# Routing and scattering one group ahead of the shared experts in a transformer-block kernel

## What is computed

```python
shared_out = einsum(silu(x @ shared_gate) * (x @ shared_up), shared_down)   # every token, width 256
router_probs = softmax(x @ router)                                          # 8 experts
topk_probs, topk_idx = top_k(router_probs, 2)
...
expert_out = (silu(x @ experts_gate[e]) * (x @ experts_up[e])) @ experts_down[e]
routed = sum over the two chosen experts of prob * expert_out
return routed + shared_out                                                  # x is the layer norm of the stream
```

## Time and profile before

| | before |
|---|---|
| median of 3 runs | 942.51 us |
| lowest, highest | 940.07, 943.23 us |
| the profiled execution, its own time | 942.55 us |
| its span, first to last instruction | 940.7 us |
| mean granted clock of TensorE | 0.942 |
| expert groups, first routing product to the first quad transpose | 234.3 to 379.48 us |

### The profile page before, as it was taken

How to read it: one execution, slowest core, us unless ns; L and a number is a source line. 1 busy time by engine, 2 the same in 40 slices (tenths; PEclk the granted TensorE clock), 3 DMA queues, 4 the chain that set the end, 5 groups by cost and what they waited for, 6 DMA issues and landing times. The chain is left out here.

```text
span 940.7 us, 24231 instructions
## 1 busy us (share of the span) xinstructions
PE 825.0 (88%) x9252; PEld 687.1 (73%) x9252; DVE 720.6 (77%) x1407; ACT 628.3 (67%) x1170; POOL 577.6 (61%) x666
## 2 busy tenths in 40 slices
PE   5699999998988786788888859999998889999995
PEld 4588888887867676778887748888877745555663
DVE  3699998887755655557565478999989968999996
ACT  2488888875633420656555128988787759999995
POOL 2355878653335344155555478879998877777551
PEclk9799999999989988799889959999999989999997
DMA  8500111000112115455443386500110320004000
GB/s 261 104 3 2 48 47 36 3 2 2 45 51 84 60 69 184 123 149 176 142 147 123 129 290 92 88 6 3 23 27 2 46 36 18 29 24 84 29 29 28
DMA packets 48481, 66.88 MB, mean 71 GB/s; under 512 B 10097, under 2 KB 36337, under 8 KB 48369
## 3 DMA queue, kind: packets, MB, share of 16 engines
q1 hardware_dynamic: 31520, 36.97, 13.3%
q0 software_dynamic: 15232, 27.80, 11.7%
q10 hardware_dynamic: 1616, 0.58, 0.3%
HBM read 35.04 MB, written 26.10 MB: 65 GB/s over the span
## 5 line engine op out<-in xcount | busy, mean ns | idle before, releaser
L568 POOL TENSOR_TENSOR sm_a<-sm_a,mx_a 128x1232 f32<-128x1232 f32 x64 | 144.0, 2250 | 84.4 <-DVE mx_a L968 84.2
L1258 POOL DMA_INDIRECT mixed<-rep,qidx_f x80 | 79.5, 994 | 82.9 <-DVE rep L1770 62.8
L968 DVE TENSOR_REDUCE mx_a<-sm_a 128x16 f32<-128x1232 f32 x64 | 91.9, 1436 | 2.2
L735 PE MATMUL pT_a<-ident,pr_a 128*128 128x128 f32 x640 | 92.1, 275 | 1.1 <-ACT pr_a L869 1.1
L869 ACT ACTIVATE pr_a<-sm_a 128x1232 f32<-128x1232 f32 x64 | 79.0, 1235 | 12.0 <-POOL sm_a L568 12.0
L1252 POOL DMA_INDIRECT slots<-sx,idx_f x48 | 47.3, 985 | 64.4 <-DVE idx_f L1656 51.6
L735 PEld LDWEIGHTS pT_a<-ident,pr_a 128*128 128x128 f32 x640 | 75.0, 142 | 2.9 <-ACT pr_a L869 1.9
L759 PE MATMUL pA_a<-aw,ot_a 128*128 128x256 f32 x256 | 66.2, 381 | 0.9 <-DVE x L986 0.9
L1949 PE MATMUL pS<-b,dg 128*128 128x512 f32 x124 | 60.2, 609 | 4.0 <-PEq L446 4.0
L961 DVE TENSOR_TENSOR sm_a<-pS_a,mask 128x1232 f32<-128x1232 f32 x32 | 46.1, 1441 | 11.7 <-PE pS_a L721 9.1
L750 PE MATMUL pO_a<-rep,V 128*32 128x128 f32 x1024 | 52.2, 276 | 1.6 <-DVE ot_a L981 1.6
(11 more groups left out here) (356 smaller groups left out, 2681.4 us busy)
## 6 DMA issues: line engine op xcount, KB each, us to landing
sx<-slots SPq DMA_DIRECT2D x40, 272.0 KB
x<-x_in SPq DMA_DIRECT2D x4, 1024.0 KB, 11.4
x<-mixed POOLq DMA_DIRECT2D x4, 1024.0 KB, 10.0
out_x<-x SPq DMA_DIRECT2D x32, 128.0 KB, 1.7
rep<-gu_in SPq DMA_DIRECT2D x10, 256.0 KB, 2.9
slots<-zeros_f SPq DMA_DIRECT2D x9, 272.0 KB
aw<-aw_in SPq DMA_DIRECT2D x2, 1024.0 KB, 7.2
ha<-mixed SPq DMA_DIRECT2D x2, 1024.0 KB, 7.4
```

Of the source, the lines that this page charges most:

```text
L568: pool.tensor_tensor(heads, heads, mx[u][:].rearrange("p (h a) -> p h a", a=1).broadcast_to([P, HEADS, SK]), ALU.subtract).then_inc(shifte ...
L735: mm = pe.transpose(pT[:, (J * t + j) % 2, (n % 4) * P:(n % 4 + 1) * P], pr[u][:, g, c * P:(c + 1) * P], sb["ident"][:])
L968: dve.tensor_reduce(mx[u][:], sm[u][:].rearrange("p (h k) -> p h k", k=SK), AX.X, ALU.max).then_inc(maxed, 1)
L1258: pool.indirect_dma_start(dram["mixed"][:], bass.IndirectOffsetOnAxis(qidx[:, at:at + 1], 0), ys[q % 2][:, j, :], None).then_inc(out_moved ...
```

## The change

Routing and scattering are moved one group ahead of the shared experts. Period s now holds the shared experts of s, the turning of s+2, and the ranking, finding and addresses of s+1; the routing product of s+2 ends it. In a longer opening, groups 0 and 1 are both routed beside shared group 0. The last period has shared work alone. For that there are three sets of turned rows and four of rows to scatter. The third turned set and the rows' middle two lie where the quads' weights `wb` come later, so ACT waits for the scatters of groups 5 and 6 before the second copy. The weights of quads 0 and 1 are copied before the quads begin. SP's zero fills are moved ahead of its waits for group 6. DVE computes the table before the products of group 7, and makes the columns `bvb` behind the last `add`. The filler calls between the last down products are gone; the 14 behind them remain. `choose` is split into `rank_of` and `choose`.

```diff
@@ -37,7 +37,7 @@
 AHEAD = 2
-THIRDS = 3
+ROWSETS, XSETS = 4, 3
 NG = T // ST
@@ -1163,8 +1163,11 @@
 qidx = sbt("qidx", [P, NQ * ST], mybir.dt.uint32)
-with nc.sbuf_tensor("rows_third" + tag, [P, ST, ROW], F32) as third:
-    rows = [*sx, third]
+with ExitStack() as groups:
+    own_set = lambda n, shape, d: groups.enter_context(nc.sbuf_tensor(n + tag, shape, d))
+    xh, xl = ([sb[n + "_first"], second, own_set(n + "_third", [P, G, GW], F32R)]
+              for n, second in (("xh", xh_second), ("xl", xl_second)))
+    rows = [sx[0], *(own_set(n, [P, ST, ROW], F32) for n in ("rows_second", "rows_third")), sx[1]]
 wb = pair("wb", [P, 2, 2 * G * D], F32R)
@@ -1209,12 +1212,12 @@
-    sp.sem_inc(rows_free, THIRDS * ST)
+    sp.sem_inc(rows_free, ROWSETS * ST)
     for g in range(NG):
-        if g == NG - 1:
+        if g == NG - 2:
             tails()
         for j in range(ST):
-            sp.wait_ge(moved[g % THIRDS][j], 16 * TOPK * (g // THIRDS + 1))
+            sp.wait_ge(moved[g % ROWSETS][j], 16 * TOPK * (g // ROWSETS + 1))
             sp.sem_inc(rows_free, 1)
@@ -1289,7 +1293,8 @@
-    def find(g, u, last=False):
+    def find(g, last=False):
+        u = g % 2
         pe.wait_ge(sel_ok, g + 1)
@@ -1329,35 +1334,52 @@
-    def group(s, u):
-        turn(s + 1, 0)
-        gate_up(s, u, 0, 1)
-        gate_up(s, u, 1, 0)
-        turn(s + 1, 1)
-        gate_up(s, u, 1, 1)
-        find(s, u)
-        turn(s + 1, 2)
+    def turn_ahead(s, j):
+        if s + 2 < NG:
+            turn(s + 2, j)
+
+    def group(s):
+        turn_ahead(s, 0)
+        gate_up(s, 0, 0)
+        if s + 1 < NG:
+            route_back(s + 1)
+        gate_up(s, 0, 1)
+        turn_ahead(s, 1)
+        gate_up(s, 1, 0)
+        turn_ahead(s, 2)
+        gate_up(s, 1, 1)
+        if s + 1 < NG:
+            find(s + 1, s + 2 == NG)
         down(s, 0)
-        turn(s + 1, 3)
+        turn_ahead(s, 3)
         down(s, 1)
-        route(s + 1, 1 - u)
-        gate_up(s + 1, 1 - u, 0, 0)
-        route_back(s + 1)
-
-    route(0, 0)
+        if s + 2 < NG:
+            route(s + 2)
+
+    route(0)
+    turn(1, 0)
     pe.wait_ge(sb["split_low"], PIECES)
-    gate_up(0, 0, 0, 0)
+    gate_up(0, 0, 0)
     route_back(0)
-    for s in range(NG - 1):
-        group(s, s % 2)
-    gate_up(NG - 1, 1, 0, 1)
-    gate_up(NG - 1, 1, 1, 0)
-    find(NG - 1, 1, True)
-    gate_up(NG - 1, 1, 1, 1)
-    keep_busy(pe, sb, pX, 4)
-    down(NG - 1, 0)
-    keep_busy(pe, sb, pX, 10)
-    down(NG - 1, 1)
+    turn(1, 1)
+    gate_up(0, 0, 1)
+    turn(1, 2)
+    find(0)
+    turn(1, 3)
+    route(1)
+    turn(2, 0)
+    gate_up(0, 1, 0)
+    route_back(1)
+    turn(2, 1)
+    gate_up(0, 1, 1)
+    find(1)
+    turn(2, 2)
+    down(0, 0)
+    turn(2, 3)
+    down(0, 1)
+    route(2)
+    for s in range(1, NG):
+        group(s)
     keep_busy(pe, sb, pX, 14)
@@ -1487,36 +1510,59 @@
     def norm_ahead(s, j):
+        if s + 3 < NG:
+            norm(s + 3, j)
+
+    def high_ahead(s, j):
         if s + 2 < NG:
-            norm(s + 2, j)
-
-    def group(s, u):
-        x_high(s + 1, 1 - u, 0)
+            x_high(s + 2, j)
+
+    def group(s):
+        if s + 1 < NG:
+            logits_out(s + 1)
+        high_ahead(s, 0)
+        norm_ahead(s, 0)
         silu(s, 0)
-        soft(s)
-        norm_ahead(s, 0)
-        x_high(s + 1, 1 - u, 1)
+        high_ahead(s, 1)
+        if s + 1 < NG:
+            soft(s + 1)
         high(s, 0)
+        high_ahead(s, 2)
+        norm_ahead(s, 1)
         silu(s, 1)
-        norm_ahead(s, 1)
-        x_high(s + 1, 1 - u, 2)
+        norm_ahead(s, 2)
         high(s, 1)
-        norm_ahead(s, 2)
-        x_high(s + 1, 1 - u, 3)
+        high_ahead(s, 3)
         norm_ahead(s, 3)
-        logits_out(s + 1)
...
     logits_out(0)
+    x_high(1, 0)
     for j in range(1, ST):
         norm(1, j)
-    for s in range(NG - 1):
-        group(s, s % 2)
-    silu(NG - 1, 0)
-    soft(NG - 1)
-    high(NG - 1, 0)
-    silu(NG - 1, 1)
-    high(NG - 1, 1)
+    x_high(1, 1)
+    silu(0, 0)
+    soft(0)
+    x_high(1, 2)
+    high(0, 0)
+    norm(2, 0)
+    norm(2, 1)
+    x_high(1, 3)
+    norm(2, 2)
+    norm(2, 3)
+    logits_out(1)
+    x_high(2, 0)
+    x_high(2, 1)
+    soft(1)
+    silu(0, 1)
+    x_high(2, 2)
+    high(0, 1)
+    norm(3, 0)
+    x_high(2, 3)
+    for j in range(1, ST):
+        norm(3, j)
+    for s in range(1, NG):
+        group(s)
@@ -1545,11 +1591,18 @@
             quad_high(q + 2, u, 1)
-            gate_up_weights(q + 2, u)
+            if q >= 0:
+                gate_up_weights(q + 2, u)
         if has(1):
...
     act.wait_ge(table_ok, 1)
+    gate_up_weights(0, 0)
+
+    for g in (NG - 3, NG - 2):
+        for j in range(ST):
+            act.wait_ge(moved[g % ROWSETS][j], 16 * TOPK * (g // ROWSETS + 1))
+    gate_up_weights(1, 1)
     run_quads(step)
@@ -1611,6 +1665,9 @@
         dve.tensor_reduce(rank[:], gt[:], AX.X, ALU.add).then_inc(r_chain, 1)
+
+    def choose(g):
+        r, u = R * g, g % 2
         dve.wait_ge(r_chain, r + 7)
@@ -1672,39 +1729,66 @@
-    def group(s, u):
-        compare(s)
-        x_low(s + 1, 1 - u, 0)
-        choose(s, u)
+    def group(s):
+        x_low(s + 2, 0)
+        compare(s + 1)
+        rank_of(s + 1)
         product(s, 0)
-        x_low(s + 1, 1 - u, 1)
-        describe(s)
+        x_low(s + 2, 1)
+        choose(s + 1)
+        x_low(s + 2, 2)
         low(s, 0)
+        describe(s + 1)
         product(s, 1)
-        x_low(s + 1, 1 - u, 2)
-        places(s)
+        places(s + 1)
         low(s, 1)
-        shares(s)
-        x_low(s + 1, 1 - u, 3)
-        addresses(s)
+        shares(s + 1)
+        x_low(s + 2, 3)
+        addresses(s + 1)
         add(s)
...
-    for s in range(NG - 1):
-        group(s, s % 2)
+    x_low(1, 0)
+    compare(0)
+    rank_of(0)
+    x_low(1, 1)
+    choose(0)
+    product(0, 0)
+    x_low(1, 2)
+    describe(0)
+    places(0)
+    low(0, 0)
+    shares(0)
+    x_low(1, 3)
+    addresses(0)
+    x_low(2, 0)
+    compare(1)
+    rank_of(1)
+    x_low(2, 1)
+    choose(1)
+    product(0, 1)
+    x_low(2, 2)
+    describe(1)
+    places(1)
+    low(0, 1)
+    shares(1)
+    x_low(2, 3)
+    addresses(1)
+    add(0)
+    for s in range(1, NG - 2):
+        group(s)
     compare(NG - 1)
-    choose(NG - 1, 1)
+    rank_of(NG - 1)
+    choose(NG - 1)
+    product(NG - 2, 0)
     describe(NG - 1)
+    low(NG - 2, 0)
     shares(NG - 1)
...
     addresses(NG - 1)
-    product(NG - 1, 0)
-    low(NG - 1, 0)
-
-    dve.wait_ge(sb["att_in"][1], 16 * 4)
-    for k in range(G):
-        last = dve.tensor_scalar(bvb[k], sb["ones"][:], bqkv[:, 2, k:k + 1], None, ALU.mult)
-    last.then_inc(s_bvb, 1)
+    product(NG - 2, 1)
+    low(NG - 2, 1)
+    add(NG - 2)
@@ -1729,9 +1813,16 @@
     dve.tensor_scalar(tab_w[:], owner[:], float(WC), None, ALU.mult).then_inc(table_ok, 1)
+    product(NG - 1, 0)
+    low(NG - 1, 0)
     product(NG - 1, 1)
...
     add(NG - 1)
+
+    dve.wait_ge(sb["att_in"][1], 16 * 4)
+    for k in range(G):
+        last = dve.tensor_scalar(bvb[k], sb["ones"][:], bqkv[:, 2, k:k + 1], None, ALU.mult)
+    last.then_inc(s_bvb, 1)
```

More of the change, by code:

```diff
@@ L1141, in moe_phase @@
         lg = sbt("lg", [P, GW])
-        xh, xl = ([sb[n + "_first"], sbt(n + "_second", [P, G, GW], F32R)] for n in ("xh", "xl"))
+        xh_second, xl_second = (sbt(n + "_second", [P, G, GW], F32R) for n in ("xh", "xl"))
         sg, hf = pair("sg", [P, GW]), pair("hf", [P, GW])
@@ L1252, in _ @@
                         pool.indirect_dma_start(dram["slots"][:], bass.IndirectOffsetOnAxis(idx[:, at:at + 1], 0),
-                                                rows[g % THIRDS][:, j, :], None).then_inc(moved[g % THIRDS][j], 16)
+                                                rows[g % ROWSETS][:, j, :], None).then_inc(moved[g % ROWSETS][j], 16)
             for q in range(NQ):
@@ L1275, in turn, with route @@
                 for k in range(G):
-                    mm = pe.transpose(pX[:, k * P:(k + 1) * P], rows[g % THIRDS][:, j, k * P:(k + 1) * P], sb["ident"][:])
+                    mm = pe.transpose(pX[:, k * P:(k + 1) * P], rows[g % ROWSETS][:, j, k * P:(k + 1) * P], sb["ident"][:])
                 mm.then_inc(xt_ps, 1)
-            def route(g, u):
+            def route(g):
+                u = g % XSETS
                 pe.wait_ge(xl_ok, ST * g + ST + 1)
@@ L1304, in find, with gate_up @@
                 mm.then_inc(place_ps, 1)
-            def gate_up(s, u, c, a):
-                n = 2 * s + c
+            def gate_up(s, c, a):
+                n, u = 2 * s + c, s % XSETS
                 pe.wait_ge(xl_ok, ST * s + ST + 1)
@@ L1455, in norm, with x_high @@
                 act.wait_ge(rows_free, t + 1)
-                act.activation(rows[g % THIRDS][:, j, 0:D], X[:, piece(t, D)], ACT.Identity, scale=RS[:, bass.ds(t, 1)],
+                act.activation(rows[g % ROWSETS][:, j, 0:D], X[:, piece(t, D)], ACT.Identity, scale=RS[:, bass.ds(t, 1)],
```

(14 more changed lines are left out.)

## The result

| | before | after |
|---|---|---|
| median of the runs | 942.87 us (4 runs, 940.07 to 943.61) | 934.16 us (4 runs, 927.69 to 941.82) |
| ratio, with its 95% interval | | 0.9884 (0.9849 to 0.992) |
| the profiled execution, its own time | 942.55 | 930.5 |
| batch 0, batch 1 start | 247.81, 262.79 | 247.78, 261.71 |
| batches 1 to 6 | 84.54 | 73.33 |

The ratio is of fast runs, without the run of 941.82, which lies 1.5% above the fastest; the two medians alone would give 0.991. So the change is about 1.2% faster where no change was forecast, and of the 11.9 us between the two spans 11.2 lie in five periods of the groups' stage. (Of the rest, the start gave 1.1; the quads took 2.3 longer, and what follows them 1.9 less, for neither of which the forecast had a term. A slip in the text ahead of the prediction: there are twenty quads, not ten. Nothing in the sum used the number.)

The account below looks back on a forecast made before the run. It took the group loop as bound: scatter batch, PE's hand-overs seen only about 11.35 us in, then the remaining steps, not busy time. Terms -0.3 -0.1 +0 +2.5 -1.1 = +1.0 gave 943.5 us, range 934 to 949.5.

Parts of the forecast that it names:

- (a): Start, up to batch 1: batch 0 at 247.1, batch 1 at 262.5 instead of 262.79; -0.3 us, trusted within 1.5.
- (b): Batches 1 to 6: three periods of 17.6 and two of 15.8 make 84.4 us, against 84.5; -0.1.
- all early: Lower bound for the five periods of batches 1 to 6: 79.0 us, with transpose 2 in time in every group.
- (c): Batch 6 to 7: find 7 still late behind all four gate products, so 12.7 us stays; 0.
- (d): Batch 7 to first quad transpose: PE's queue with group 7's work and fourteen fillers ends at 21.9, not 19.46; +2.5 us.
- gate 0 in time: Alternative for batch 7 to the first quad transpose: group 7's gate 0 not late, giving 20.5 us, +1.0.
- (e): First quads: they start at full clock, but quad 2's load lands 8.5 after the start against 9.66; -1.1 us.
- In time: Rival, 0.26: transpose 2 leaves early in every group; periods sum to 79.0, total 938.2, or 935.7 with quad at load's end.
- Free of the scatter: Rival, 0.07: scatters do not hold PE's hand-overs; 62.5 us for the five periods, 22 less, total 921.5.
- The tail binds: Rival, 0.22, slower: PE's queue between last down product and quad 0 decides; 947.6 us, or 950 with all periods late.
- no real lead: Rival, 0.07: find 1 late in the first batch, so everything slips back into the old phase; 942 us.
- The rule: Against the predicted loop: scatters would not hold PE's hand-overs; five periods of 12.5 us against 84.5 in batches 1 to 6.

Follow-up runs that it names:

- a_none_again: Changed kernel without the scatters of groups 1 to 7 and the quads' loads, quads scattering to made-up rows, on a chip that holds signals: 916.2 us.
- b_none_again: Kernel before without the scatters of groups 1 to 7 and the quads' loads, quads scattering to made-up rows, on a chip that holds signals: 912.4 us.
- a_tail: Changed kernel with its end undone: fillers between group 7's down products, later table, earlier bv columns, first quads' weights copied in the loop: 943.6 us, 0.9936 of before.
- a_quads: Changed kernel with a 128x256 Pool fill behind each scatter of groups 1 to 6 and all quads but the last: 915.1 us, 1.0377 of before.

## Why the prediction was wrong

It forecast 943.5 us, no change, where 934.2 was measured.

**(a) Start**, -0.3 forecast: -1.1 measured (batch 0 at 247.78 for 247.1, batch 1 at 261.71 for 262.5), within its 1.5.

**(b) Five periods**, -0.1 forecast: -11.2 measured, 73.3 us, below the bound of 79.0 "all early". This step failed, in two sentences. "If the route ends 0.95 into the batch ... only silu 1 is late: the same 4.5 remain, 15.8": that was so in the first of the five periods, with silu 1 at 11.33 and a period of 15.85. In the other four the route ended about 1.3 in, and transpose 2 left in time, but silu 1 started at 9.2 to 10.0, not at 11.35. I had made a fixed window, 7.7 to 11.35, of signals that were all let go at its end (and set its start too late: my own row has one held that ended 7.33 in). In those four a signal that ends 7.28 in is seen at once, one at 8.68 is 0.5 to 1.3 late, and only find's waits to the end; why these differ from the old order's, where the one at 7.33 waited to 11.3, is open. And "PE then idles some 3 us ... and runs it and the route at the lower clock": it idled 1.35 ahead of down 1 and kept the full clock (1.00 in the windows), so no period of 17.6 followed. A bound was missing: the rest behind a hand-over that alone stays late, places to batch. I had the pieces for it, 0.6 for shares and 1.37 from the last low half on.

The frame of the loop held: the period is the end of the hold, 11.4 to 11.5, and what remains behind it. What I had wrong is which signals are held how long, and so what remains: 3.0 us, not 4.5 or 5.9 to 6.5. My own sign, "wrong if the spacing is under 15 (the late stretch is not bound to the scatter)", came true with 14.1 to 14.5, but what it was to show did not follow: the stretch is bound to the scatter, and the spacing fell because less stood behind it. That the scatters make the hold was an inference; a_none_again and b_none_again show it.

**(c) Batch 6 to 7**, 12.7 forecast, 12.65 measured.

**(d) Batch 7 to the first quad transpose**, 21.9 forecast, 19.88 measured. The alternative "gate 0 in time", 20.5, was the case: silu 0 of group 7 started 7.67 in. PE's fillers ended at 19.6, and the quad waited 0.3 us for its load:

```profile
363.97 3.29 PE L159 MATMUL pX_f<-ident 128*128 128x128 f32 x28
367.57 0.63 PE L1395 MATMUL pX_f<-ident,sx 128*128 128x128 f32 x4 [0.32 <-DMA sx<-slots]
```

I counted the table ahead of group 7's products as a delay; in a_tail, with it behind product 0, the first quad turns 3.4 us later. By its trace some 2 of them come from this and from the bv columns (0.5) ahead of the table; the two were not taken apart.

**(e) The first quads**, -1.1 forecast. Quad 2 was turned 8.44 us behind quad 0 (8.5 forecast, 9.66 before), waiting for its load as forecast:

```profile
376.01 0.68 PE L1395 MATMUL pX_f<-ident,sx 128*128 128x128 f32 x4 [1.82 <-DMA sx<-slots]
```

But PE was busy for only 5.95 of the 9.4 us up to 377.0, its clock was 0.80 from there to 384.4, and 0.8 us of the gain went back. (d) and (e) together: 0, for +1.4.

**The rivals.** *In time* had the right sign and nearly the size (935.7 with the first quad at its load), but by periods of 15.8, of which the new order has one; that the size is near is luck. *Free of the scatter* was given 0.07 and is how this kernel behaves in two sets of six, with periods of 13.3. *The tail binds* was wrong, *no real lead* too, since the periods are shorter; and the slowing that exists was not on my list: the new order's own 0.8 us a period.

**The rule.** The Trainium skill ("SBUF - State Buffer", section "Who interferes with whom") says that a DMA never contends with a compute engine. On the chips where nothing is held, the new order's traces agree: five periods of 66.4 us with the scatters and 66.5 without. On the others PE's passes of 512 columns follow one another in 0.23 us at the full clock, beside scatters as in the execution without held signals, so PE itself is not slowed; it is its signals that arrive up to some microseconds late while Pool scatters, and the rule as stated does not cover that.

## What to carry to other kernels

Before restructuring around a wait that the profile calls "remote", compare the end of the producer with the start of its reader all over the trace, and see what else runs where they part; then try the cheap cure at the suspected cause. Here 0.2 us between scatters gave in the old order at least what a new schedule with one more set of each buffer gave, and the best version had both: on a chip that holds signals 0.977 of before, on one that doesn't about 0.3% slower (one run of each). Measure a schedule change, too, on more than one chip: this one is worth 1.2 to 1.4% on some and nothing on others, because it moves signals out of a hold and pays 0.8 us a period for it.

## What the runs showed of the hardware

- The same kernel takes 943 to 949 us in four sets and 882 to 884 in two. The quads' stage is 135 to 139 us on the first and 100 to 104 on the others, at the same scatters (133.5 with the fills of a_quads). What sets the chips apart is open.
- PE's signals were late only while indirect DMAs of 128 rows ran: in no execution was one of the 275 to 277 ahead of them late, and at most one of some 320 to 375 behind.
- The hold goes by the closeness of the scatters and not by their bytes: rows of 64 bytes hold like rows of 1088, two runs of four 3.0 us apart held nothing (seen once), and with a step of 1.46 instead of 1.26 us five periods take 69.3 us instead of 83.1 to 84.5. What it consists of is open.
- Held are signals of PE alone, and in the same stretches a fifth to a third of the raises by DVE and ACT have no record; where nothing is held, next to none is missing.
